# The scaling of y in a layer norm: one VectorE operation becomes a ScalarE activation and two small ones

## What is computed

```python
x = x + _L0_conv_ref(_gn(x), ...)   # first block
x = x + _L1_conv_ref(_gn(x), ...)   # second block
```

```python
y = _chunk_scan(x, dt, A, Bm, Cm) + D[None, None, :, None] * x
y = y.reshape(B, L, D_INNER)
mu = jnp.mean(y, axis=-1, keepdims=True)
var = jnp.var(y, axis=-1, keepdims=True)
y = (y - mu) / jnp.sqrt(var + EPS) * norm_w + norm_b
y = y * z
out = y @ out_proj_w.T
```

## Time and profile before

| | |
|---|---|
| median of 3 runs | 3477.97 us (3474.12 to 3478.38) |
| the profiled execution | 3468.43 us, its span 3466.7 us |
| PE busy | 2881.6 us, 83% |
| DVE busy | 2827.0 us, 82% |
| ACT busy | 1853.7 us, 53% |
| POOL busy | 1554.3 us, 45% |
| granted TensorE clock, mean | 0.911 |

### The profile page before, as it was taken

The page is one execution under the profiler, slowest core; times in us unless marked ns, Lnnn a source line. Parts: engine busy times, 40 slices in busy tenths (PEclk is TensorE's granted clock), DMA queues, the critical chain, the costliest instruction groups (busy, mean ns, idle before and its releaser), DMA issues. The chain is left out here.

```text
span 3466.7 us, 61986 instructions
## 1 busy us (share of the span) xinstructions
PE 2881.6 (83%) x20640; PEld 1535.8 (44%) x20640; DVE 2827.0 (82%) x4364; ACT 1853.7 (53%) x4379; POOL 1554.3 (45%) x1107
## 2 busy tenths in 40 slices
PE   3788888988888888888888888888888988888865
PEld 2554445354443635445354443535445354443510
DVE  1458979798797978979698796978979798897997
ACT  1647474653747456464654746456374654636542
POOL 2115544444444444444344444444444444444455
PEclk8999999998999999999999999989899999989976
DMA  2042141423215142231423214142231424214131
GB/s 58 17 116 71 66 112 53 116 71 109 76 47 149 38 138 71 82 102 46 117 71 115 81 48 137 38 137 71 72 107 53 116 71 122 80 45 132 37 113 58
DMA packets 104168, 291.02 MB, mean 84 GB/s; under 512 B 25373, under 2 KB 27020, under 8 KB 103820
## 3 DMA queue, kind: packets, MB, share of 16 engines
q1 hardware_dynamic: 103820, 286.71, 27.6%
HBM read 181.84 MB, written 39.85 MB: 64 GB/s over the span
## 5 line engine op out<-in xcount | busy, mean ns | idle before, releaser
L749 POOL TENSOR_TENSOR hc<-hst,bcrep 128x512 f32<-128x512 f32 x768 | 1212.5, 1579 | 1291.8 <-DVE hst L1246 1263.3
L1295 PE MATMUL bank<-hc,sel 128*32 128x512 f32 x1536 | 431.6, 644 | 113.0 <-POOL hc L749 109.2
L1233 DVE TENSOR_TENSOR wr<-durep,bcrep 128x512 f32<-128x512 f32 x768 | 520.6, 678 | 2.5 <-DMA bcrep<-bc_rows 2.5
L837 ACT ACTIVATE ssd<-bank,ncs 128x128 f32<-128x128 f32 x1536 | 439.4, 386 | 107.6 <-PE bank L1295 107.1
L1246 DVE TENSOR_TENSOR_SCAN hst<-dec,wr 128x512 f32<-128x512 f32 x256 | 390.8, 1527 | 99.1 <-ACT carry L981 71.2
L940 ACT ACTIVATE bank<-durep,aneg 128x512 f32<-128x512 f32 x368 | 252.6, 690 | 194.1 <-DVE hst L1246 149.8
L1295 PE MATMUL bank<-xna,wt0a 128*128 128x128 f32 (+3 forms) x1088 | 315.7, 395 | 45.1 <-DVE xnb L1046 31.7
L1246 DVE TENSOR_TENSOR_SCAN hst<-bank,carry,wr 128x512 f32<-128x512 f32 x240 | 306.5, 1277 | 14.5 <-ACT bank L940 4.8
L1295 PE MATMUL bank<-ssd,wcv 64*32 64x512 f32 (+1 forms) x6144 | 308.1, 544 | 0.0
L1295 PE MATMUL bank<-xnb,wt0b 128*128 128x128 f32 (+3 forms) x1088 | 302.8, 383 | 0.0
L940 ACT ACTIVATE dec<-durep,aneg 128x512 f32<-128x512 f32 x400 | 291.1, 733 | 7.0 <-DVE hst L1246 4.7
(11 more groups left out here) (187 smaller groups left out, 5006.3 us busy)
## 6 DMA issues: line engine op xcount, KB each, us to landing
durep<-scratch SPq DMA_DIRECT2D x192, 512.0 KB, 3.9
bcrep<-bc_rows SPq DMA_DIRECT2D x128, 512.0 KB, 5.1
ssd<-stage SPq DMA_DIRECT2D x384, 140.4 KB, 2.9
ssd<-bcst SPq DMA_DIRECT2D x128, 74.4 KB, 2.6
xa<-in_x_dram SPq DMA_DIRECT2D x16, 512.0 KB, 3.9
scratch<-u SPq DMA_DIRECT2D x32, 256.0 KB, 2.1
scratch<-delta SPq DMA_DIRECT2D x32, 256.0 KB, 2.8
out_dram<-x1a SPq DMA_DIRECT2D x16, 512.0 KB, 4.8
```

What stands on the lines that cost most here:

```text
L749: nc.gpsimd.tensor_tensor(hc[:, i % CRING, :], hst[:, i % HRING, :], bcrep[:, g, 1, :], ALU.mult).then_inc(hc_ready.sem, 1)
L837: ins = nc.scalar.activation(att[:, c % 2, h, :], bank[ROW_BANKS[r]][:, k * Q:(k + 1) * Q], ACT.Exp, bias=ncs[:, c, h:h + 1])
L1233: nc.vector.tensor_tensor(wr[:, i % WRING, :], durep[:, j % SLOTS_DU, 1, :], bcrep[:, g, 0, :], ALU.mult).then_inc(w_made.sem, 1)
L1295: return nc.tensor.matmul(out, lhsT, rhs, start=start, stop=stop, skip_group_check=True)
```

## The change

VectorE's normalise is gone. VectorE makes lnm = -mean instead, one element for each position, ahead of lve. GpSimd, after its power, waits for it and makes lmr = lnm * lrs. ScalarE applies y0 = y0 * lrs + lmr as one activation, in stage 5, behind its copy of the transposed x, and signals TensorE.

```diff
         lrs = sb("lrs", [P, 2])
+        lmr = sb("lmr", [P, 2])
+        lnm = sb("lnm", [P, 2])
...
             def layer_rstd(n, c):
                 pool.wait_ge(lve_ready.sem, lve_ready.at(n, c + 1))
-                nc.gpsimd.tensor_tensor(lrs[:, c % 2:c % 2 + 1], lve[:, c % 2:c % 2 + 1], neghalf[:, 0:1],
-                                        ALU.pow).then_inc(lrs_ready.sem, 1)
+                k = slice(c % 2, c % 2 + 1)
+                nc.gpsimd.tensor_tensor(lrs[:, k], lve[:, k], neghalf[:, 0:1], ALU.pow).then_inc(lrs_ready.sem, 1)
+                pool.wait_ge(lrs_ready.sem, lrs_ready.at(n, c + 1))
+                nc.gpsimd.tensor_tensor(lmr[:, k], lnm[:, k], lrs[:, k], ALU.mult).then_inc(lmr_ready.sem, 1)
...
                     nc.scalar.copy(xtok[:, c % 2, :], bank[B_XY][:, :]).then_inc(xt_copied.sem, 1)
+                c = chunk_at(s, 5)
+                if c >= 0:
+                    act.wait_ge(lmr_ready.sem, lmr_ready.at(n, c + 1))
+                    nc.scalar.activation(y0[:, c % 2, :], y0[:, c % 2, :], ACT.Identity, bias=lmr[:, c % 2:c % 2 + 1],
+                                         scale=lrs[:, c % 2:c % 2 + 1]).then_inc(ynorm_ready.sem, 1)
...
                 step(nc.vector.bn_aggr(lmv[:, c % 2, :], lst[:, c % 2, :]))
+                nc.vector.tensor_scalar(lnm[:, c % 2:c % 2 + 1], lmv[:, c % 2, 0:1], -1.0, None, ALU.mult)
                 nc.vector.tensor_scalar(lve[:, c % 2:c % 2 + 1], lmv[:, c % 2, 1:2], LEPS, None, ALU.add).then_inc(lve_ready.sem, 1)
-
-            def normalise(n, c):
-                dve.wait_ge(lrs_ready.sem, lrs_ready.at(n, c + 1))
-                nc.vector.tensor_scalar(y0[:, c % 2, :], y0[:, c % 2, :], lmv[:, c % 2, 0:1], lrs[:, c % 2:c % 2 + 1],
-                                        ALU.subtract, ALU.mult).then_inc(ynorm_ready.sem, 1)
...
-                c = chunk_at(s, 5)
-                if c >= 0:
-                    normalise(n, c)
```

More of the change, by code:

```diff
@@ L360, in build @@
         lrs_ready = sig("lrs_ready", NCH)
+        lmr_ready = sig("lmr_ready", NCH)
         ynorm_ready = sig("ynorm_ready", NCH)
```

## The result

The changed kernel takes 3379.73 us (median of 4 runs, 3373.93 to 3382.05), the kernel before 3476.05 beside it (median of 4, 3473.64 to 3478.38): a ratio of 0.972 (0.9704 to 0.9737), 96 us less. The profiled executions stand at 3382.05 and 3468.43, 86.4 apart; what follows explains those 86.4. The other 10 lie in the choice of executions: the profiled one of before was faster than all of its four timed ones.

The account below looks back on a forecast made before the run. VectorE bounds the chunk stage at 10.65 to 11 us a chunk, TensorE right behind at 10.36. Chunk gains of 5.84 us less 0.3 give 5.5 per image; 15 images make 83: 3478 - 83 = 3395, range 3355 to 3440.

Parts of the forecast that it names:

- Chunk 0, worth 0: Start of an image's chunk stage: normalisation is short, VectorE idles 2.01 us for TensorE right behind it; gain 0.
- Chunks 1 to 4, worth 1.5 by TensorE's loop: Middle chunks: VectorE falls under TensorE's loop of 10.36 us, which then sets the time; 42.5 against 44.15, worth 1.5.
- Chunk 6, worth 1.7 less 0.1: Late chunk: TensorE's transposes can start at 1610.0 instead of 1611.75, worth 1.7 us; VectorE's added operation costs 0.1.
- Chunk 7, worth 1.3 less 0.1: Last chunk: chunk 6's pattern without VectorE's idle 1.25 us, worth 1.3; VectorE's added operation costs 0.1.
- The rest passed on: After chunk 7: VectorE's and TensorE's own work releases all, so the gain of 5.5 us per image should be passed on.
- the second rival: Gain given back behind the chunks or by uneven co-bound pieces: only chunks 5 to 7 pay, 38 us, 3440; chance 0.2.
- The first image, worth 0, at worst -0.8: First of 16 images: chunks run beside no scan and VectorE has gaps; counted 0, at worst 8 x 0.1 us.
- GpSimd's small product, 0.54 + 0.05: 128x1 product behind GpSimd's power: 0.54 us plus 0.05 wait; free in chunks 2 to 4, on the path in 6, 7.
- ScalarE's activation, 0.64, with a cover of 0.3: 128x384 activation takes 0.64 us; 0.3 is left between the exponentials' end and L870's start, hiding it from TensorE's loop.
- VectorE is the bound everywhere: Rival: TensorE catches up as its waits shrink; all 134 us less 13 gained, 121 us, 3357; chance 0.12.
- ScalarE blocks: Rival, slower: VectorE disturbs GpSimd's small product, 3.0 us long, delaying ScalarE; loops pay from 1.45; +105 us, 3583; chance 0.06.
- ScalarE's length counts: Rival, slower: ScalarE's queue is on the path, 0.64 against VectorE's 0.46 per chunk, 23 us, 3501; chance 0.02.

Follow-up runs that it names:

- the last experiment: Changed kernel again, beside itself with TensorE's own-state product moved ahead of the product of C and B: 3380.11 us (ratio 0.973) and 3383.47 us (0.9751).
- the 0.341 of bn_stats: Changed kernel plus an unused 128x192 bn_stats on VectorE, one input, at the old normalisation's place in chunks 1 to 4: 3390.62 us in one run.
- the best version here that stays on VectorE: Kernel before with only normalise moved in VectorE's queue, ahead of the scan unit instead of behind it: 3411.09 us, ratio 0.9815.
- with the own state first: Changed kernel with TensorE's product for a chunk's own state moved ahead of the product of C and B: 3381.90 us, ratio 0.975; again 3383.47, 0.9751.
- the 128x192 product of two SBUF inputs: Changed kernel plus an unused VectorE multiplication at the old normalisation's place: 3406.04 us in chunks 1 to 4, 3432.66 in chunks 5 to 7.

## Why the prediction was right

It said 3395 in a range of 3355 to 3440, and it came to 3380. The mechanism was right in the middle of the chunk stage, where TensorE's loop takes over from VectorE. The close sum, 83 us against 86 between the profiled executions, is in part luck. Up to the first xna behind the chunks an image won 7.4 us in place of 5.5, some 28 us more than forecast over 15 images; behind it 1.4 an image came back and the first image lost 3.4, some 25 us. By its own steps:

- **Chunk 0, worth 0.** 0.07. Right, although GpSimd's product took 1.86 there: nobody on the path waited for it.
- **Chunks 1 to 4, worth 1.5 by TensorE's loop.** 1.61. Right in size and in cause: the loop is 10.36, VectorE waits for TensorE ahead of y0, and moving one product on TensorE shortens the loop only since the change. The wait is small, 0.07 in the mean and 0.21 at most, and it is released by TensorE ahead of L1101, not by ScalarE ahead of the attention product, where the prediction looked for it. The short price of 0.92 holds for chunks 2 to 4; in chunk 1 normalise took 1.42 as in the last three, which the prediction did not read.
- **Chunk 5, worth 1.34 less 0.1.** 1.24. Right.
- **Chunk 6, worth 1.7 less 0.1.** 2.47, and here two terms were off. The transposes came 1.16 earlier after bn_stats (4.62 before, 1607.13 to 1611.75; 3.46 after, 1574.97 to 1578.43) and not some 1.7, since the small product took 0.94 and not 0.54. But from the transposes to y0 it went 2.67 instead of 4.14 (1578.43 to 1581.10, against 1611.75 to 1615.89), for the six gate products ran at twice the clock. Before:

```profile
1612.44:1615.01 2.57, 2.57 (x14) 2.57 (x14) 2.20 (x4) 1.74 (x4) 0.80 (x1) 0.50 0.01 3
```

After:

```profile
1578.81:1580.15 1.34, 1.34 (x14) 1.34 (x13) 1.34 (x4) 1.28 (x5) 0.56 (x1) 1.00 0.00 0
```

  The granted clock is 0.50 (1.2 GHz) in the first, behind 3.74 us in which TensorE idled, and 1.00 (2.4 GHz) in the second, behind 1.49. The prediction took the length of the gate products from before and did not ask why they were slow.
- **Chunk 7, worth 1.3 less 0.1.** 1.97. In the image of the rows it is 1.31 (from bn_stats to the gate product 6.66 before, 1616.48 to 1623.14; after 5.35, 1581.68 to 1587.03), and there the gate products ran at 1.00 in both kernels. In 8 of the images 1 to 14 of before they took 2.06 to 2.56 and not 1.34; in the changed kernel it is 1.34 in all, behind chunk 6 and behind chunk 7. Two images of before:

```profile
1621.48:1622.83 1.35, 1.35 (x15) 1.35 (x14) 1.35 (x2) 1.14 (x4) 0.04 (x1) 1.00 0.04 12
586.35:588.91 2.56, 2.56 (x14) 2.56 (x13) 1.50 (x2) 1.74 (x4) 1.48 (x1) 0.50 0.00 0
```

- **The rest passed on.** Not quite: of 7.4 us an image 1.2 came back between the two xna, for the most part in four images in which the stretch took over 30, at a granted clock of 0.85 to 0.86, and did not in the kernel before. This is what the second rival said in substance, at 0.4 of its size (it took 3.0 of 5.5 an image back). In the second execution of the changed kernel, made for the last experiment, it was 0.7.
- **The first image, worth 0, at worst -0.8.** It lost 3.4, all of it behind its chunks (108.08 to 112.05 up to the next chunk 0). About half of this is scatter: in the second execution of the changed kernel the same distance is 108.86. There the first image lost 1.7, of it 0.9 in its chunks, still twice the worst case. Six of its periods are 0.06 to 0.07 longer than before and the last 0.56 (5.56 against 5.00): where no scan runs beside the chunks, the longer way over GpSimd and ScalarE is on the path. What makes the 108.86 of one execution the 112.05 of the other stays open.
- **VectorE's added operation, 0.1.** Its row is 0.154 long, and the next starts 0.07 after it. Right.
- **GpSimd's small product, 0.54 + 0.05.** 0.19 where nothing disturbed it, 0.94 in chunk 6, 1.86 in chunk 0. The value from the nearest row was wrong in both directions, and too low in chunk 6, where a gain was reckoned from it.
- **ScalarE's activation, 0.64, with a cover of 0.3.** 0.71, and the cover was 0.17 in chunks 2 and 3 (at 1537.99); in chunk 4, where a copy of y1b joins the queue, it was gone and TensorE waited 0.30 for the exponentials (at 1559.15). The term was 0.07 short and about half of the cover was left. A further 0.5 us on ScalarE brought the periods up by 0.1 to 0.4.
- **The rivals.** "VectorE is the bound everywhere" is refuted for the middle chunks by the 0.341 of bn_stats that cost nothing there. "ScalarE blocks" needed a product of 1.45 in chunks 1 to 4; it was 0.19. "ScalarE's length counts" would be seen in the kernel without the normalisation; its periods are the same. The Trainium skill's advice to use VectorE for additions and multiplications ("ScalarE: Activation LUTs", section "Rules for kernel authors") holds here for the work itself (0.46 against 0.71), but not for the time of the kernel: the move to ScalarE wins 2.8%, and the best version here that stays on VectorE 1.85%.

What the prediction did not see at all is why normalise was dear. It took 1.00 and 1.42 as the price of the operation and noted 0.46 as its shortest; the difference was the wait for GpSimd's running instruction, and the move of normalise within VectorE's own queue gets 63 of the 94 us by which the changed kernel won on the same chip. The terms for VectorE came out right because the edit took away work and wait together.

## What to carry to other kernels

When the same instruction has several durations in a trace, ask what the other engine is doing beside each before moving its work: a place in the same queue where GpSimd is idle was worth two thirds of what the move to a third engine was (63 of 94 us). Where two engines are bound within 0.3 us of each other, work out the loop of the second before counting the gain of the first, and check it by an edit to the second one's queue. And a gap that closes on TensorE can pay twice, through the clock of what stands behind it (2.57 to 1.34 in chunk 6), while a lower clock elsewhere takes some of it back; judge a small edit by periods as well as by the total.

## What the runs showed of the hardware

- The 128x384 scale and shift from SBUF to SBUF and the 128x192 product of two SBUF inputs end 0.22 us behind the GpSimd instruction that they waited for: 1.00 and 1.42 in place of 0.46 for the first, 0.97 and 1.43 for the second (0.34 in the first image, where it was not held up). A longer operation ends later behind it: the 128x1024 scale and shift in the kernel before, 0.81 alone, took 1.75 beside GpSimd's product, and ended 0.55 behind it (rows below). bn_stats (one input) is not held up, and neither is an operation that reads one of its two inputs from PSUM (y0, 0.55 beside GpSimd's product at 376.51, 0.54 alone).

```profile
1021.14 1.33 POOL L749 TENSOR_TENSOR hc<-hst,bcrep 128x512 f32<-128x512 f32 x1
1021.27 1.75 DVE L1045 TENSOR_SCALAR xna<-x1a,gm,gr 128x1024 f32<-128x1024 f32 x1
```

- Not every operation that finds GpSimd under way is held up: in chunk 0 of before normalise took 0.46 although GpSimd's record had begun 1.84 earlier.
- It goes the other way too. GpSimd's one-column product, 0.19 alone, took 0.94 from 1576.69 and ended at 1577.63, 0.03 ahead of the end of VectorE's scan (1576.38 + 1.28); in chunk 0 it took 1.86 and ended at 1512.48, 0.06 behind VectorE's scan and the product behind it, although its own record begins 0.02 ahead of the scan's:

```profile
1510.64 1.21 DVE L1249 TENSOR_TENSOR_SCAN hst<-dec,wr 128x512 f32<-128x512 f32 x1
1511.77 0.65 DVE L1236 TENSOR_TENSOR wr<-durep,bcrep 128x512 f32<-128x512 f32 x1
...
1576.38 1.28 DVE L1249 TENSOR_TENSOR_SCAN hst<-dec,carry,wr 128x512 f32<-128x512 f32 x1
```

- The stretch of the same 80 products of TensorE takes 26.7 us in one image and 30.6 in another, at a granted clock of 0.97 and 0.85, and the gate products 1.34 or 2.56 at 1.00 or 0.50. The clock is not all of it: in the changed kernel the stretch took from 26.5 to 29.7 at 0.96 to 0.98. In a kernel whose edits are worth 1 to 2 us an image, this decides as much as they do.
- How long TensorE idled does not by itself tell the clock behind it. In chunk 6 the gate products ran at 1.00 behind 1.49 us of idleness and at 0.50 behind 3.74; with the own state first, behind 1.81 to 1.90 in all 15 images, they took 2.15 to 2.27 in six of them and 1.34 in the other nine.
